# A gated two-layer block on one core: time-mix scans moved behind the routes' entry, and a multiply given to GpSimd

## The reference, cut to what matters

```python
x = x + tanh(g_xattn[0]) * wkv(time_decay, time_first, k=layernorm(x), v=ctx)      # time mix
...
# first feed-forward block, on layernorm(x)
scores, pk = top_k(all_scores, 8); indices = take_along_axis(all_idx, pk)          # routes
ew = einsum('nh,nkh->nk', x, down_embed[indices])
ew = silu(ew) * softmax(scores)
experts_states = einsum('nk,nkh->nh', ew, up_embed[indices])
mlp = silu(x @ gate_w) * (x @ up_w) @ down_w
x = x + tanh(g_ffn[0]) * (mlp + experts_states)
...                                                   # linear attention, then a routed MoE of 8 experts, top 2
```

## Time and profile before

| | us |
|---|---|
| median of 3 runs | 519.91 |
| lowest, highest | 518.77, 523.19 |
| span of the profiled execution | 517.5 |
| TensorE busy in it | 449.8 (87%) |
| VectorE busy in it | 360.9 (70%) |
| ScalarE busy in it | 246.7 (48%) |
| GpSimd busy in it | 154.5 (30%) |

### The profile page before, as it was taken

How to read it: one execution, slowest core, us unless ns; L and a number is a source line. 1 busy time by engine, 2 the same in 40 slices (tenths; PEclk the granted TensorE clock), 3 DMA queues, 4 the chain that set the end, 5 groups by cost and what they waited for, 6 DMA issues and landing times. The chain is left out here.

```text
span 517.5 us, 7233 instructions
## 1 busy us (share of the span) xinstructions
PE 449.8 (87%) x2142; PEld 355.1 (69%) x2142; DVE 360.9 (70%) x1034; ACT 246.7 (48%) x452; POOL 154.5 (30%) x156
## 2 busy tenths in 40 slices
PE   1617999599999889999999999898999799899991
PEld 1315688368578666878778886787777588788851
DVE  6896779995289986565987966978867554531173
ACT  3618574363576346346125315470453454955540
POOL 3955342330002131110000001032336014477771
PEclk9966999799999989999999999999999999999997
DMA  8500312000300000960000000123232423346394
GB/s 303 187 31 30 103 31 83 0 1 0 101 2 0 2 0 14 310 178 0 1 1 1 1 0 2 32 71 102 90 115 83 123 73 91 114 139 208 85 385 153
DMA packets 32965, 42.00 MB, mean 81 GB/s; under 512 B 3483, under 2 KB 26781, under 8 KB 32928
## 3 DMA queue, kind: packets, MB, share of 16 engines
q1 hardware_dynamic: 28224, 32.28, 20.7%
q0 software_dynamic: 3744, 8.42, 4.4%
q10 hardware_dynamic: 960, 0.86, 0.5%
HBM read 24.97 MB, written 18.39 MB: 84 GB/s over the span
## 5 line engine op out<-in xcount | busy, mean ns | idle before, releaser
L660 PE MATMUL acc<-w_down,act_s 128*128 128x256 f32 x384 | 92.2, 387 | 0.9 <-DVE act_s L1386 0.9
L660 PEld LDWEIGHTS acc<-w_down,act_s 128*128 128x128 f32 x384 | 74.6, 195 | 13.2 <-DVE act_s L1386 1.3
L636 PE MATMUL ring<-xt_h,up_l 128*128 128x512 f32 x160 | 70.5, 441 | 2.9 <-DVE xt_l L1356 1.5
L1601 POOL TENSOR_TENSOR rstd<-var_eps,minus_half 128x4 f32<-128x4 f32 x14 | 14.9, 1068 | 176.5 <-DVE var_eps L1186 176.5
L637 PE MATMUL ring<-xt_l,up_h 128*128 128x512 f32 x160 | 63.8, 399 | 0.0
L638 PE MATMUL ring<-xt_h,up_h 128*128 128x512 f32 x160 | 63.7, 398 | 0.0
L1098 ACT ACTIVATE act_s<-ring 128x512 f32<-128x512 f32 x48 | 28.6, 597 | 59.9 <-PE ring L638 59.6
L631 PE MATMUL ring<-small,xn 128*128 128x128 f32 x160 | 23.6, 297 | 26.2 <-ACT xn L998 14.1
L699 PE MATMUL ring<-up_e,act_s 128*128 x184 | 44.3, 383 | 2.3 <-issue 2.0
L1637 POOL DMA_INDIRECT x_rows<-main_a,slots x32 | 31.1, 971 | 43.7 <-ACT main_a L1119 34.8
L1390 DVE TENSOR_TENSOR act_s<-ring,act_s 128x512 f32<-128x512 f32 x32 | 22.0, 686 | 30.8 <-PE ring L638 21.0
(11 more groups left out here) (275 smaller groups left out, 987.8 us busy)
## 6 DMA issues: line engine op xcount, KB each, us to landing
main_b<-x_rows SPq DMA_DIRECT2D x22, 257.0 KB, 2.8
x_rows<-v_t SPq DMA_DIRECT2D x1, 3983.5 KB, 16.7
up_l<-y_rows SPq DMA_DIRECT2D x5, 512.0 KB, 7.0
stage<-in_w_mlp SPq DMA_DIRECT2D x8, 256.0 KB, 2.6
up_e<-in_w_moe SPq DMA_DIRECT2D x8, 256.0 KB, 2.6
x_rows<-v_t SPq DMA_DIRECT2D x1, 1927.5 KB, 22.8
x_nat<-in_x SPq DMA_DIRECT2D x7, 256.0 KB, 7.7
out_x<-x_nat SPq DMA_DIRECT2D x6, 256.0 KB, 5.2
```

The lines of the kernel that those rows point to most:

```text
L636: pe.matmul(out, wl, xh, start=first, stop=False, skip_group_check=True)
L660: last = pe.matmul(acc[t // 2][:, t % 2, :], act_s[n % RING][:, tok], w_down[:, u, :], start=u == 0 and t % 2 == 0, stop=final, skip_group ...
```

## The change

Two things are changed. The steps of `wkv_out 2` and `wkv_out 3` stand later in the table for mains 0 and 1. In units 8 to 10 of every main GpSimd multiplies `act_s` by the column weight (EY), and VectorE multiplies `act_s` in place by the rank test and by EX; unit 11 stays as it was.

```diff
 ("mlp", 0):
-        6: "route 0 7 8, wkv_out 2 0",
-        7: "wkv_out 2 1",
-        8: "peer_in 0 0, wkv_out 2 2 3",
-        9: "wkv_out 2 4 5, kv 1 0",
-        10: "wkv_out 2 6 7, x_stats 2 0, kv 1 1",
-        11: "mlp_in 1 0, kv 1 2",
-        12: "mlp_in 1 1",
+        6: "route 0 7 8",
+        8: "peer_in 0 0, wkv_out 2 0 1",
+        9: "kv 1 0, wkv_out 2 2 3",
+        10: "kv 1 1, wkv_out 2 4 5",
+        11: "kv 1 2, wkv_out 2 6 7, x_stats 2 0, mlp_in 1 0",
+        12: "mlp_in 1 1, kv 1 3 4",
 ("mlp", 1):
-        1: "mlp_out 0 0, kv 1 3 4, route 1 0, kv 2 0",
+        1: "mlp_out 0 0, route 1 0, kv 2 0",
...
-        7: "wkv_out 3 2 3",
-        8: "peer_in 1 0, wkv_out 3 4 5",
-        9: "kv 3 0",
+        8: "peer_in 1 0, wkv_out 3 2 3",
+        9: "kv 3 0, wkv_out 3 4 5",
         10: "wkv_out 3 6 7, x_stats 3 0, kv 3 1",
```

VectorE, units 8 to 11:

```diff
                         if HID_TURN[("mlp", g, u)] > 1:
                             dve.wait_ge(hid_ready, HID_TURN[("mlp", g, u)] - 1)
 
-                        bank = full(dve, (step, "RANK", u))
-                        free((step, "RANK", u), dve.scalar_tensor_tensor(w, bank[:, :], float(TOPK), host_s[:, 0, :],
-                                                                         ALU.is_gt, ALU.mult))
-                        bank = full(dve, (step, ("EX", u)))
-                        free((step, ("EX", u)), dve.tensor_tensor(w, w, bank[:, :], ALU.mult))
-                        if u == MLP_UNITS - 1:
+                        if u < MLP_UNITS - 1:
+                            dve.wait_ge(values_scaled, (MLP_UNITS - 1 - IC) * g + u - IC + 1)
+                            bank = full(dve, (step, "RANK", u))
+                            free((step, "RANK", u), dve.scalar_tensor_tensor(s[:, :], bank[:, :], float(TOPK), s[:, :],
+                                                                             ALU.is_gt, ALU.mult))
+                            bank = full(dve, (step, ("EX", u)))
+                            free((step, ("EX", u)), dve.tensor_tensor(s[:, :], s[:, :], bank[:, :], ALU.mult))
+                            dve.sem_inc(hid_ready, 1)
+                            continue
+                        else:
+                            bank = full(dve, (step, "RANK", u))
+                            free((step, "RANK", u), dve.scalar_tensor_tensor(w, bank[:, :], float(TOPK), host_s[:, 0, :],
+                                                                             ALU.is_gt, ALU.mult))
+                            bank = full(dve, (step, ("EX", u)))
+                            free((step, ("EX", u)), dve.tensor_tensor(w, w, bank[:, :], ALU.mult))
                             bank = full(dve, (step, "OVER"))
                             free((step, "OVER"), dve.tensor_tensor(w, w, bank[:, :], ALU.add))
```

GpSimd:

```diff
                     pool.wait_ge(past_added, C * g + c + 1)
                     pool.wait_ge(recip_ready, C * g + c + 1)
                     pool.tensor_tensor(y, y, by_token(ee_a[c][:, 1, :]), ALU.mult).then_inc(y_ready, 1)
+                elif kind == "mlp" and IC <= part - 1 < MLP_UNITS - 1:
+                    s = act_s[unit_of(g, part - 1) % RING]
+                    freed(pool, (step, "EY"))
+                    freed(pool, (step, "A", part - 1))
+                    pool.tensor_tensor(s[:, :], s[:, :], host_s[:, 0, :], ALU.mult).then_inc(values_scaled, 1)
                 elif kind == "split":
                     split_low(part)
                 elif kind == "qg":
```

More of the change, by code:

```diff
@@ L465, in build @@
         hid_ready = sem("hid_ready")
+        values_scaled = sem("values_scaled")
         down_done = sem("down_done")
```

## The result

In one session the changed kernel took **537.92 us** (median of 4 runs, 536.65 to 538.79) and the kernel before 521.22 us (518.77 to 523.19): ratio 1.0319, 95% interval 1.0289 to 1.0348, 16.6 us slower. The forecast was 532.0, with a range of 522 to 541. The profiled executions stand 19.5 us apart in span (537.0 and 517.5). Some 3 us of that are scatter: the profiled run of before was at the low end of its runs, that of the change (538.79) at the high end. Two of the three experiment sessions ran at another level, where the kernel before itself took 536.1 and 538.2 us, so ratios are taken only within a session.

The account below looks back on a forecast made before the run. TensorE, busy 87% of the span, was taken to bound the kernel by standing or running at lower clock. Mains 0 to 3 gave 3 + 2 + 0 + 7 = +12 us; 519.9 + 12 = 532 us, range 522 to 541.

Parts of the forecast that it names:

- Part 1, the entries: Mains 0 and 1: `exps_t_l` starts ahead of the scans or reciprocals, 5.0 us earlier at 91.1 and 3.6 earlier at 178.0.
- the 12.6 us "if nothing is given back": Mains 0 and 1: the earlier entries' 5.0 and 3.6 us plus 2.3 and 1.7 us of low clock avoided.
- Part 2, main 0: Moved work and VectorE's waits for GpSimd's multiply use up the entry's 5.0 us; with low clock, +3 us (0 to +6).
- The two stands: Main 0, units 9 and 10: VectorE stands each time for two GpSimd instructions of 1.27 us, +5.1 us in all.
- that overlap: Main 0: GpSimd's multiply of unit 8 beside VectorE's scans, costing up to 1.0 us, within main 0's bounds.
- Part 2, main 1: Time-mix transposes wait until 192.5, TensorE stands 5.2 us with low clock behind; the 3.6 us are gone, +2 us (0 to +5).
- Part 3, main 2: VectorE's idle time hides unit 8's 1.6 us delay there; 0 us taken (0 to +2).
- Part 4, main 3: Unit 8's multiply queues behind four sends, TensorE stands 5.5 us plus about 1.8 of low clock: +7 us (+5 to +9).
- Unit 10's multiply, which "may cost another": Main 3: this multiply waits for sends whose rows ScalarE scales after copying the transposes; a possible further cost, given no size.
- the contention rival: Chance 0.11: the twelve multiplies and VectorE's work beside them each pay about 0.8 us more, 10 us in all: 542.
- The queue of sends: Rival, chance 0.15: in main 3 it does not reach TensorE, which loses 1 us at most: about 525.
- The entry's gain: Rival, chance 0.12: it survives, mains 0 and 1 keep up to 12.6 us: 514, or 507 if main 3 is spared.

Follow-up runs that it names:

- e1_order: The changed kernel's new step order alone, no multiply on GpSimd: 533.99 us where the kernel before took 536.09, ratio 0.9957.
- e3_main3: The changed kernel with the three products of units 8 to 10 back on VectorE in main 3 alone: 543.14 us, ratio 1.0137 to the kernel before.
- e9_q01: New order, GpSimd's multiply in mains 0 and 1 only, queued ahead of the time mix's pair; mains 2 and 3 as before: 520.83 us, ratio 0.9992.
- e7_queue: The changed kernel with main 3's sends later and GpSimd's multiply ahead of the time mix's pair in mains 0 and 1: 522.86 us, ratio 1.0031.
- e8_fill: The changed kernel with 28 overwritten matmuls put into TensorE's stand ahead of main 3's transposes: 543.75 us, ratio 1.0423 to the kernel before.
- e6_order0: The kernel before with the new order in main 0 alone, no multiply on GpSimd: 520.76 us where before took 520.92, ratio 0.9989.
- e5_sends: The changed kernel with main 3's sends behind parts 8, 9 and 10 put one part later: 542.45 us, ratio 1.0144 to the kernel before.
- f3_kv: New order, main 1's time-mix transposes later, GpSimd multiplying in main 0 alone ahead of the pair, one kv step ahead of main 0's transposes: 525.62 us, ratio 0.9784.
- e2_mult: GpSimd's multiply in units 8 to 10 of all mains, in the order of the kernel before: 548.27 us, ratio 1.0239.

## Why the prediction was right, point by point

- **Part 1, the entries.** Main 0: 91.1 said, 90.85 measured. Main 1: 178.0 and main 0's +3, 181.97 measured. Right. But the 12.6 us "if nothing is given back" did not need GpSimd's multiply to be lost: the order alone kept 2.3 of them (e1_order), with TensorE standing at the time mix's transposes.
- **Part 2, main 0**, +3 (0 to +6). Main 1's entry came 4.0 us after the 178.0; e3_main3, the same kernel up to here, would give 2.3, so the split between mains 0 and 1 is only good to 1.7 us, their sum to 0.6. The two stands were 2.72 us each, for 2 x 1.27; `rstd` 1.20, for 1.1; `xn` ended at 124.4, for 123.1. Nearly all of this 1.3 is unit 8's stand of 1.18 us. The forecast had bounded that overlap at 1.0 us, from a case in which GpSimd got in after one scan; here it got in only after three, 2.8 us fell on its multiply, and VectorE waited. TensorE stood 3.12 + 1.06 + 1.00 + 3.25 = 8.4 us (9.3 said), with the low clock behind the first and the last.
- **Part 2, main 1**, +2. Transposes 196.5 (192.5 and main 0's 4.0), 197.09 measured; stand 5.2, measured 5.68; main 2's entry 5.9 late less 4.0 is 1.9. Right, within the 1.7 us above. But the wait for GpSimd is not the only thing that takes the entry's gain: with the order alone (e1_order) and with the multiply out of that queue (e9_q01) TensorE stood for the same transposes.
- **Part 3, main 2**, 0 (0 to +2): measured 1.0 (97.58 for 96.61), again in e7_queue against e9_q01 (97.50 for 96.65). Inside the bounds, not the value taken.
- **Part 4, main 3**, +7 (+5 to +9): the mechanism was right, the term too small, and the measured 10.1 lies outside its bounds. Unit 8 was done at 385.8, for 378.6 + 6.9 = 385.5. `xn` was done at 388.7, for 386.9: one of its instructions was held up 1.3 us by unit 9's multiply, which the forecast did not have. So the stand was 7.3 us (5.5 said), and the clock behind it cost 2.7 (1.8 said). That is 10.0, the 10.1 of the trace; e3_main3 gives 9.5 by the ratio. Unit 10's multiply, which "may cost another", did wait for the late sends, and VectorE for it (6.36 us). The unit was done at 397.8, 0.5 us before the gate scores began, so this cost nothing here. It is the next limit (e8_fill).
- **The sum.** 3 + 2 + 0 + 7 = 12 said; 4.0 + 1.9 + 1.0 + 10.1 = 17.0 at the gate scores. The 16.6 us of the ratio fit that. The further 2.5 us of the span, behind the gate scores (138.7 us for 136.3), are no more than scatter: e6_order0 and e9_q01, which have the instructions and the order of before there, took 137.7 and 139.9. A stretch at 0.65 around 425 us lies among them (eight matmuls took 3.67 us, 1.99 before), but in e9_q01 the same eight took 3.78. In all, three terms were low, by 1.0, 1.0 and 3.1 us, and none was high by more than 0.1. The number alone would not have told the forecast (532) from the contention rival (542): 537.9 lies between them, and only the experiments decide.
- **The rivals.** The queue of sends reached TensorE (e3_main3, e5_sends). The entry's gain did not survive, though it can (f3_kv). Contention as a price on each multiply fell: the 12 took 18.0 us in sum, 2.8 more than 12 x 1.27, all in one. But two single overlaps did reach TensorE, 1.2 us by unit 8 of main 0 and 1.3 by `xn` of main 3, together 2.5 of the 4.1 us by which the forecast was low in these two mains.

## What to carry to other kernels

Before a piece of work goes to an idle engine, read what stands ahead of it in that engine's queue, and what that waits for. The same multiplies cost main 3 some 8.5 to 10.1 us behind four sends and 1.1 to 2.4 ahead of them (e5_sends against e3_main3, e7_queue against e9_q01). An engine that waits for its helper holds its own queue too: main 3's loss was `xn` standing behind VectorE's wait, and the clock after it. And work that comes early gains nothing until the next meeting point moves with it. Here the order alone gave 2.3 us, one step moved in main 1 made it 5.6, and with the multiply in main 0, ahead in its queue, and one more step moved it was 11.6.

## What the runs showed of the hardware

- **VectorE and GpSimd block each other for whole instructions.** Beside VectorE's four scans (4.59 us) GpSimd's multiply took 4.03 us instead of 1.27 (4.00 to 4.03 in seven other kernels) and ended 1.1 us behind the last scan, and the scans themselves were not longer (1.20 to 1.22 us each). The other way round, an `xn` instruction of VectorE beside a multiply of GpSimd that had begun took 1.70 us, median 0.41. Line L1200 in the changed kernel (duration ns min/median/max, first and last start):

```profile
L1200 DVE TENSOR_SCALAR xn<-x_nat,mv,rstd x44: 401/408/1698, 7.9 to 455.3; 128x256 f32<-128x256 f32 x44
```

The Trainium skill (SBUF — State Buffer, "SBUF: two separate sides") says of VectorE instructions with two inputs from SBUF, or in a two-port mode, that whichever of VectorE and GpSimd starts first gets the shared port pair for its whole instruction, and the other waits. The `xn` case agrees with that (1.70 us for 0.41, and 2.07 in e2_mult). The forecast took only the kind with two inputs into account; `xn` reads one tensor and was held up too. Who comes next where one instruction of VectorE ends and another begins is not told by it, and went both ways: in the changed kernel the third and fourth scans began on time, though the multiply had been waiting since the second. In the kernel before, GpSimd's add (92.32) got in after the first of two scans, and the second took 2.24 us instead of 1.23.

- **A send did not do that** in the one case seen: `xn` beside one took 1.38 us for its four instructions (e5_sends).
- **The clock's price**: 2.7 us behind a stand of 7.3; a clock of 0.64 for 4.7 us behind one of 3.1, which is 0.36 x 4.7 = 1.7 us. With stands of 2.5 and 1.6 us at most (f3_kv) the stretch of 42 us around them had 1.00. It is not the same in every execution: e3_main3, the same kernel up to main 2, kept 1.00 for 7.3 us behind the same stand of 3.1, and ran at 0.52 from 118 to 124 us, after one of 2.7. The 1.7 us by which its distance from main 0 to main 1 is shorter are of this size, though that is not shown to be the reason.
